# Issuing the memory and output-projection weight strips from ScalarE's queue instead of SyncE's in an eight-core linear-attention layer

## What is computed

```python
q = hidden_states @ w_q.T; k = hidden_states @ w_k.T; v = hidden_states @ w_v.T
sigma_q = elu_plus_one(q)
a_mem = sigma_q @ memory
norm = jnp.clip(sigma_q @ memory_norm, EPS, None)[..., None]
memory_output = active * (a_mem / norm)
# causal linear attention, chunks of 128 tokens:
#   num = (sq sk^T * mask) v + sq S_kv ; den likewise with z ; S_kv += sk^T v
g = jax.nn.sigmoid(gate)
output = g * memory_output + (1.0 - g) * local_output
return output @ w_o.T
```

## Time and profile before

| what | value |
|---|---|
| time, median of 2 runs | 5216.82 us (5068.16 to 5365.47) |
| time of the profiled execution | 5068.51 us |
| span of its slowest core (core 7) | 5067.0 us |
| spans of the 8 cores | 5013.4 to 5067.0 us |
| P2 on core 7 | from 1720 to 3360 us |
| busy shares of core 7 | PE 53%, DVE 34%, ACT 25%, POOL 4% |
| mean granted TensorE clock, core 7 | 0.771 |

### The profile page before, as it was taken

How to read it: one execution, slowest core, us unless ns; L and a number is a source line. 1 busy time by engine, 2 the same in 40 slices (tenths; PEclk the granted TensorE clock), 3 DMA queues, 4 the chain that set the end, 5 groups by cost and what they waited for, 6 DMA issues and landing times. The chain is left out here.

```text
span 5067.0 us, 34731 instructions; the slowest of 8 cores (5013.4 to 5067.0 us)
## 1 busy us (share of the span) xinstructions
PE 2691.8 (53%) x10855; PEld 1123.3 (22%) x10855; DVE 1705.1 (34%) x2399; ACT 1257.0 (25%) x1457; POOL 222.6 (4%) x203
## 2 busy tenths in 40 slices
PE   1120565564746457757755766742236556457465
PEld 1010122221212123213322322310012222223222
DVE  3332333343252323322322332325433422432433
ACT  1211233323323232023122123111123223133131
POOL 0000000000000011011111111000000000000000
PEclk8555778787878788988988888875568778678687
DMA  4554101001000221321331231232120010000000
GB/s 127 156 178 134 61 1 67 0 17 50 1 33 1 87 44 40 90 60 38 79 83 34 75 83 42 50 100 69 59 93 0 17 50 0 31 36 1 34 1 34
DMA packets 358787, 272.81 MB, mean 54 GB/s; under 512 B 271541, under 2 KB 273617, under 8 KB 358610
## 3 DMA queue, kind: packets, MB, share of 16 engines
q1 hardware_dynamic: 347090, 239.13, 16.1%
q10 hardware_dynamic: 11520, 31.46, 2.0%
HBM read 192.96 MB, written 77.59 MB: 53 GB/s over the span
## 5 line engine op out<-in xcount | busy, mean ns | idle before, releaser
L206 PE MATMUL p1pH<-p1xnp,p1cw 128*128 128x512 bf16 x1536 | 401.0, 429 | 159.7 <-ACT p1xnp L97 87.2
L206 PE MATMUL p4pH<-p4xnp,p4cw 128*128 128x512 bf16 x1536 | 398.6, 427 | 153.4 <-ACT p4xnp L97 84.9
L206 PEld LDWEIGHTS p1pH<-p1xnp,p1cw 128*128 128x128 bf16 x1536 | 163.0, 108 | 402.4 <-issue 266.1
L206 PEld LDWEIGHTS p4pH<-p4xnp,p4cw 128*128 128x128 bf16 x1536 | 162.6, 108 | 394.3 <-issue 256.7
L206 PE MATMUL ptr<-idf,x0t 128*128 128x128 f32 x256 | 58.6, 402 | 339.8 <-DVE stg L97 179.8
L97 DVE TENSOR_SCALAR p4crow<-row,c 1x512 bf16<-1x512 f32 x24 | 12.8, 533 | 637.0 <-ACT row L97 637.0
L206 PE MATMUL pA_<-xn_p,wq_strip 128*128 128x512 bf16 x512 | 137.6, 421 | 168.5 <-DVE xn_p L97 108.3
L97 DVE TENSOR_SCALAR p1crow<-row,c 1x512 bf16<-1x512 f32 x24 | 12.8, 533 | 618.1 <-ACT row L97 618.1
L97 ACT ACTIVATE row<-row 1x512 f32<-1x512 f32 x80 | 50.2, 628 | 662.1 <-DVE row L97 659.8
L206 PE MATMUL p1pG<-p1h,p1cw 128*128 128x512 bf16 (+1 forms) x816 | 183.8, 379 | 57.6 <-ACT p1h L97 57.6
L206 PE MATMUL p4pG<-p4h,p4cw 128*128 128x512 bf16 (+1 forms) x816 | 183.8, 379 | 56.9 <-ACT p4h L97 56.9
(11 more groups left out here) (218 smaller groups left out, 4399.0 us busy)
## 6 DMA issues: line engine op xcount, KB each, us to landing
x_sb<-x2f SPq DMA_DIRECT2D x12, 2048.0 KB, 9.6
x0t<-hs SPq DMA_DIRECT2D x8, 2048.0 KB, 17.2
x0f<-stg SPq DMA_DIRECT2D x8, 2048.0 KB, 9.8
x_sb<-x1f SPq DMA_DIRECT2D x8, 2048.0 KB, 9.1
wq_strip<-awq SPq DMA_DIRECT2D x64, 256.0 KB, 3.2
wk_strip<-awk SPq DMA_DIRECT2D x64, 256.0 KB, 3.0
wq_strip<-awm SPq DMA_DIRECT2D x64, 256.0 KB, 3.2
wo_strip<-awo SPq DMA_DIRECT2D x64, 256.0 KB, 3.5
```

Source lines behind the costliest of these rows:

```text
L206: i = getattr(e, name)(*a, **kw)
```

## The change

The DMA start of each memory strip (8 per block) and of each output strip (8 per block) is issued by ScalarE in place of SyncE, with the wait for its buffer. Nothing is added or left out, and the same semaphores are counted.

```diff
@@ emit_pb
-                        @blk.sync
-                        def _(q, et=et, msl=msl, msem=msem):
-                            wm_slot[msl].wait(q)
-                            q.dma_start(
+                        @blk.scalar
+                        def _(s, et=et, msl=msl, msem=msem):
+                            wm_slot[msl].wait(s)
+                            s.dma_start(
                                 out=mem_strip[:, msl, :, :],
...
@@ emit_wo
-                        @blk.sync
-                        def _(q, b=b, ft=ft, wsl=wsl, swo=swo):
-                            wo_slot[wsl].wait(q)
-                            q.dma_start(
+                        @blk.scalar
+                        def _(s, b=b, ft=ft, wsl=wsl, swo=swo):
+                            wo_slot[wsl].wait(s)
+                            s.dma_start(
                                 out=wo_strip[:, wsl, :, :],
...
```

## The result

The changed kernel takes 5012.2 us (median of 11 runs, 4999.73 to 5192.01) against 5081.05 us (median of 10 runs, 5063.81 to 5365.47). The ratio is 0.9882 with a 95% interval of 0.9853 to 0.9912, about 60 us of the kernel before. The profiled execution took 5010.6 us against 5068.5, with a span of 5009.0 us on core 7.

What follows compares the result with a forecast made beforehand. The attention stage was taken to go at the pace of TensorE's work plus its waits. Of 73.4 us gross gain, 50.5 stayed after costs; 5068.51 less 50.5 plus 1.0 gave 5019 us, range 4988 to 5056.

Steps and rivals of the forecast that it cites:

- The waits removed: Start of blocks 1, 3, 5, 7: TensorE's four waits for memory strips, 65.55 us, go.
- The clock: First step after each of those waits runs at full clock: 1.97 us, four times, 7.9 us.
- What comes back beside store and load: Odd blocks' memory steps: 5.9 us wait plus 1.0 us clock in three pairs, 2.3 us in the last.
- 73.4 gross: Attention stage: gain from the four waits and the clock together, before the costs beside store and load.
- The other places: Pair starts cost 1 us in all; output strips 0, range -7 to +12; casts and squares stay covered.
- The sum: Whole kernel: 5068.51 of the profiled execution, less 50.5, plus 1.0, gives 5019 us.
- the marks: Signs in the changed profile: memory-strip wait about 20 us, strips 2 and 3 landing in 8 to 10, output-strip wait near 43.
- even sharing: Strips beside bulk transfers land in under 4.0 us, so no wait comes back: 4996 us, chance 0.18.
- turns by packet: DMA engines alternate between two queues, so strip 3 would not stand behind the whole load; wait nearer the lower bound.
- deep backlog: Odd blocks: strip 2 already waits until the load is through, TensorE only two steps ahead: 5034 us, chance 0.14.
- Nothing gained: Strips need the load's end on any queue, or the waits return elsewhere: 5068 us, chance 0.07.
- The slower rival: Output strips 2 to 7: longer round trip by ScalarE's queue, 24 us per us of delay; chance 0.09.

Runs made afterwards that it cites:

- held version: Changed kernel with the even block's store and following load both held until the next block's memory step is done: stage 1542.6 us, ratio 0.987.
- the first experiment: Changed kernel with the output strips back on SyncE, only memory strips issued by ScalarE: ratio 0.9913, stage 1570.8 us.
- load released mid-step: Changed kernel with the next even block's load held until the third step of blocks 1, 3, 5 is done: ratio 0.9899, stage 1564.9 us.
- reordered single list: Kernel before, all strips on SyncE, memory strips 0 and 1 of odd blocks issued ahead of the previous block's store: ratio 0.9951, stage 1582.2 us.
- reordered list: Kernel before, all strips on SyncE, even block's store and following load moved behind the next block's memory strips: ratio 0.9865, stage 1541.9 us.

## Why the prediction was right, and where it was off

**The waits removed.** 65.55 us in four pieces were to go, and all four went: no first step of an odd block waits. Strips and casts were to be ready by about 2056. The casts ended at 2054.1; the strips, issued at 2050.90 and 2051.61, landed after 5.0 and 6.0 us and not after 3.2, the first at 2055.9 and the second at 2057.6, 1.6 us late by the forecast but still ahead of its step, which starts at 2060.62. The eighth output strip had been issued 0.45 us ahead of them, at 2050.45.

**The clock.** 1.97 us per pair were to come back with it, and the first step does take 4.0 us now.

**What comes back beside store and load.** This is the term that was mis-sized. The prediction put 5.9 us of wait and 1.0 us of clock on each of three pairs, for a strip 3 behind the load, and 2.3 us on the last, together 23.0 us. By the same bookkeeping (73.4 gross less 58.2 measured in the four pairs) it was 15.2 us, and its shape was different. Strip 3 stands behind the load in one pair of core 7 only, the second. Of the 24 pairs of the eight cores that have a load it is issued ahead of the load in 23, mostly by 0.5 us, and then lands after 2.9 to 4.8 us; in the one where it comes 0.2 us late it takes 9.8. I had the two at 2066.1 and 2065.9, a margin of 0.2 us that I treated as certain. It falls the other way because the store takes longer with strip 2 beside it: the load, which waits for it, is issued 7.67 us behind it instead of the 6.99 of the earlier trace rows. The price of a strip behind a load was right: 9.8 us against the 9.7 of the earlier trace rows. What was left in its place is strip 2 beside the store, which I had put at some 2 us and taken as contained in the wait for strip 3: 5.4 us to land in the first pair, a wait of 1.3 to 2.7, and in two of the four pairs a lower clock after it (3.43 and 3.48 us for 8 matmuls, at 2066.74 and 2852.15), which in the first costs 1.68 of the 1.97 us that a full stop did. Nor did strips 4 and later always have the slack that I gave them: core 7 shows no such wait, but at the fifth step cores 0 and 2 wait 1.0 to 3.0 us in each pair with a load. The held version bears out the size of the term in the mean: without a bulk transfer beside the strips the stage is 15.4 us shorter. On core 7 it is 23.2, of which 13.3 are waits for memory strips and 6.5 for output strips, so that 15.2 and 15.4 agree this closely is chance. That the total came within 9 us of the forecast is in part luck too: the wait on which the largest cost was priced occurred in one pair of 24, and others that the sum did not hold took part of its place.

**The other places.** The first strips at the start of a pair were hidden, as forecast; in block 0 ScalarE issues them at 1989.83 and TensorE's step starts at 1994.52, where it was 1994.52 before. The output projection was priced at nothing with a range of -7 to +12 us: 2.3 us in the kernel that moves the output strips alone. The squares of block 2 and the casts cost nothing. What I did not see is the effect that the first experiment brought out: taking the output strips off SyncE keeps them from following the load, and this is worth 12.8 us beside the memory strips. The sum counted a bulk transfer only beside strips 2 and 3, and didn't name what keeps the one beside the later strips from being longer still.

**The sum.** 49.5 us were forecast, 57.9 measured by the profiled executions and 60 by the ratio; 5019 against 5010.6 and 5012.2. Of the marks: the memory strips' wait was to fall to about 20 (17.1 with the two pieces that carry another name), the longest to 5 or 6 (4.92), at the fourth step of three blocks (of one), strips 2 and 3 to land in 8 to 10 us (5.4 and 3.2, and 9.8 once), the output strips' wait to stay near 43 (48.5).

**The rivals.** By its mark in the prediction, strips 3 that land in under 4 us, even sharing would have held: they took 3.2 us in two of the three pairs of core 7. The mark was a poor one, since these strips were issued ahead of the load and say nothing of what one beside it costs. The load released mid-step does, with 6.4 and 6.6 us, and refutes the rival. It lay nearest in time on some cores (core 1 gained 63.6 us in the stage) for another reason, the order of two issues.

The rival argued from bytes, a strip having an eighth of the load's. The packets of the two DMA queues say why that misleads. A strip is 1040 packets and so is a load, only that the load's are eight times as long. In the second pair of core 7, changed kernel, strip 3 is issued 0.2 us behind the load; from 2461 to 2462 us SyncE's queue (q1) and ScalarE's (q10) moved, in packets and MB:

```profile
q1 hardware_dynamic: 166, 0.34, 87.2%
q10 hardware_dynamic: 170, 0.04, 19.1%
```

The turns by packet that the prediction set aside are what this shows, and they don't bring a strip through early: it needs as many turns as the load. They are not all of it. Strip 5 of the kernel with the load released mid-step, issued at 2069.73, had moved 59 of its 1040 packets by 2074, when the load was nearly through; strip 2 beside the store, issued at 2060.86, had moved none by 2064. Such a strip waits for its start, for a cause that these runs don't show. The load in P0 on which the prediction leaned shows both: ScalarE's queue moved no packet from 107 to 112 us, and then about as many as the other; also, a store of ScalarE's own, issued at 107.15, stood ahead of it.

The deep backlog, with two steps of head start, is what the reordered single list shows: 34.6 us. Nothing gained is refuted by the result itself. The sentence of the Trainium skill behind it (DMA: Bandwidth & Descriptors, "Issuing engines are not separate DMA queues") holds in these runs for the transfers: the order on one queue is as good as two queues, 1541.9 against 1542.6 us. The gain of the change lies elsewhere, in the time in which SyncE waited in its own list before it issued. The slower rival would have needed 2.1 us more per round trip and had at most 0.1.

## What to carry to other kernels

A long wait for a small transfer is first a question about its issue: find the issuing engine's own timeline and see what it waited for before it got there. Small loads that are wanted soon should not stand in one list behind a store that waits for compute and a load that waits for the store; moving them to another engine's list helps, and putting the bulk transfers behind them in the same list helped as much here and 16 us more, since it also keeps them from running side by side. When two issues lie within some tenths of a microsecond in a forecast, price both orders.

## What the runs showed of the hardware

- A 256 KB strip lands after 3.2 us (median of the earlier trace rows); most took 5.4 us when issued 3.2 us into a 2 MB store of the other queue. One took 9.8 us when issued 0.2 us behind a 2 MB load, one 6.6 us when issued 3.9 us into one: 10.0 and 10.5 us after the load's issue. 23 strips issued 0.4 us or more ahead of a load landed after 2.9 to 4.8 us.
- Two queues under way at once moved about the same number of packets in a microsecond, 166 of 2 KB and 170 of 256 bytes, so the one with short rows moved an eighth of the bytes.
- The store beside a strip pays as well: 7.5 us instead of 6.9 in the first two pairs. In the third it took 7.9 to 9.6, and about 8 in the reordered list with no strip beside it; the cause of that is open.
- ScalarE issues a DMA while the activation ahead of it in its list is still running. In the changed kernel:

```profile
1989.76 0.72 ACT L97 ACTIVATE row<-row,g_s 1x512 f32<-1x512 f32 x1
1989.83 11.87 ACTq L206 DMA_DIRECT2D wq_strip<-awm  x4
```

- The clock fell behind some short waits and not behind others: in the changed kernel 8 matmuls took 3.43 us behind a wait of 1.97 and 3.23 behind one of 4.92, but 1.89 behind waits of 1.26 and 1.94 (the rows at 2066.74, 2466.95, 2457.87 and 3242.68).
